# Attention front and step reordered around the norm chain, Newton steps of the inverse norms on GpSimd

## The reference

```python
def _features(x, omega, quad_nodes, quad_weights):
    xn = x / jnp.maximum(jnp.linalg.norm(x, axis=-1, keepdims=True), 1e-12)   # norm of each head's 16 numbers
    proj = jnp.einsum('bhtd,rhdm->rbhtm', xn, omega)
    arg = jnp.clip(proj * sqrt_2s - s, -20.0, 20.0)
    feat = jnp.exp(arg) / np.sqrt(M) * jnp.sqrt(quad_weights)
...
qkv = x @ Wqkv + bqkv
qf, kf = _features(q, ...), _features(k, ...)
# causal sums of k*v and of k over chunks of 128 rows; out = ctx / max(den, 1e-6)
return out @ Wout + bout
```

## Time and profile before

| what | value |
| --- | --- |
| median of 3 runs | 1512.48 us |
| profiled execution | 1517.87 us, span 1516.3 us |
| PE busy | 1378.1 us (91%) |
| DVE, ACT, POOL busy | 914.5, 683.9, 547.4 us |
| mixer phase ends, attention begins | 332.8 us from the span's start |
| steps 1 to 6 of attention | about 62 us each |
| attention ends, shared experts begin | about 819 us |

### The profile page before, as it was taken

The page is one execution under the profiler, slowest core; times in us unless marked ns, Lnnn a source line. Parts: engine busy times, 40 slices in busy tenths (PEclk is TensorE's granted clock), DMA queues, the critical chain, the costliest instruction groups (busy, mean ns, idle before and its releaser), DMA issues. The chain is left out here.

```text
span 1516.3 us, 33677 instructions
## 1 busy us (share of the span) xinstructions
PE 1378.1 (91%) x12000; PEld 1205.1 (79%) x12000; DVE 914.5 (60%) x1944; ACT 683.9 (45%) x1257; POOL 547.4 (36%) x503
## 2 busy tenths in 40 slices
PE   6889999959889789888897998999989999999995
PEld 5778888847667667676676987788889999999984
DVE  4757666758577676676674454344455555555547
ACT  2447756534434444444353432223245555555533
POOL 0235554442234454253410005152324444444431
PEclk7799999969989899898998999899999999999997
DMA  6233441043645545545334322543568888888885
GB/s 239 110 127 111 148 165 57 29 102 99 168 116 162 149 127 153 135 142 152 111 98 155 138 100 99 191 170 142 130 196 229 234 232 233 239 228 234 239 272 204
DMA packets 113085, 241.29 MB, mean 159 GB/s; under 512 B 21616, under 2 KB 77296, under 8 KB 105840
## 3 DMA queue, kind: packets, MB, share of 16 engines
q1 hardware_dynamic: 88768, 185.05, 39.9%
q0 software_dynamic: 23088, 54.31, 12.6%
q10 hardware_dynamic: 1152, 0.93, 0.2%
HBM read 150.23 MB, written 64.84 MB: 142 GB/s over the span
## 5 line engine op out<-in xcount | busy, mean ns | idle before, releaser
L2684 PE MATMUL ps<-e_xhl,s_whl 128*128 128x256 f32 x1848 | 246.9, 283 | 2.0 <-DMA s_whl<-wlo 2.0
L2684 PEld LDWEIGHTS ps<-e_xhl,s_whl 128*128 128x128 f32 x1848 | 232.2, 190 | 2.2 <-issue 2.2
L2066 PE MATMUL ps<-s_xhl,s_whl 128*128 128x512 f32 x660 | 170.3, 406 | 5.3 <-PEq L1127 2.6
L2515 POOL DMA_INDIRECT xs<-e_y,e_slot_id x78 | 122.0, 1564 | 89.3 <-ACT e_y L2549 70.8
L2066 PEld LDWEIGHTS ps<-s_xhl,s_whl 128*128 128x128 f32 x660 | 124.4, 194 | 34.0 <-issue 9.3
L510 POOL TENSOR_TENSOR b_hhl<-b_h,b_hhl 128x512 fp32r<-128x512 f32 x64 | 94.5, 1478 | 139.8 <-ACT b_hhl L774 118.0
L2663 PE MATMUL ps<-s_whl,e_ghl 128*128 128x256 f32 x936 | 139.9, 285 | 0.6 <-issue 0.6
L2763 DVE TENSOR_TENSOR e_g<-ps,e_act_h 128x256 f32<-128x256 f32 x156 | 66.2, 425 | 116.3 <-ACT e_act_h L2562 97.8
L2663 PEld LDWEIGHTS ps<-s_whl,e_ghl 128*128 128x128 f32 x936 | 122.6, 190 | 0.9 <-issue 0.7
L607 PE MATMUL ps<-b_w,b_hhl 128*128 128x256 f32 x768 | 105.3, 287 | 6.3 <-DVE b_turned_rows L880 5.6
L2562 ACT ACTIVATE e_act_h<-ps 128x256 f32<-128x256 f32 x156 | 59.9, 384 | 112.8 <-PE ps L2684 97.6
(11 more groups left out here) (384 smaller groups left out, 2697.2 us busy)
## 6 DMA issues: line engine op xcount, KB each, us to landing
s_whl<-wlo SPq DMA_DIRECT2D x38, 1024.0 KB, 5.1
s_fs<-s_stage SPq DMA_DIRECT2D x192, 128.0 KB, 2.4
s_whl<-wlo SPq DMA_DIRECT2D x38, 512.0 KB
c_eraw<-in_expert_w POOLq DMA_DIRECT2D x24, 512.0 KB, 5.8
wlo<-c_elo POOLq DMA_DIRECT2D x24, 512.0 KB, 3.0
wall<-in_expert_w SPq DMA_DIRECT2D x8, 1536.0 KB
xg<-b_zeros POOLq DMA_DIRECT2D x13, 780.0 KB, 3.9
e_xr<-xg SPq DMA_DIRECT2D x39, 260.0 KB
```

The lines of the kernel that those rows point to most:

```text
L2066: mm = pe.matmul(ps[:, H + 2 * (m % 2) + w, :], whl[:, wp, e, lo:lo + P], xhl[:, k, xp, kd, :], start=q == 0, stop=q == 3 * KD - 1)
L2515: gp.indirect_dma_start(xs, bass.IndirectOffsetOnAxis(ap=slot_id[:, i, b:b + 1], axis=0), y[:, k, b, :], None, compute_op=ALU.add).then_in ...
L2684: mm = pe.matmul(ps[:, H + m, w * SLOT:(w + 1) * SLOT], whl[:, k, wp, lo:lo + P], xhl[:, k, xp, kd, :], start=q == 0, stop=q == 3 * KD - 1)
```

## The change

Five edits. (1) `norm_newton` leaves VectorE; POOL gets `norm_roots` with 12 tensor_tensor on 128x128, and `norm_guess` one more instruction (the product with -0.5). (2) The slots move: FQ 1 to 3 one point earlier, FN 0 and 2 one point earlier, BW and BO 0 later; `squares` go to turn 3 (end) and turn 4 (before mask), with the guess behind the second. (3) The row chain goes from the end of turn 1 to the middle of turn 1, `normalise` from turn 2 to turn 3, `expert_high` from turns 1, 2, 3, 4 to turns 0, 1, 3, 5. (4) In the mixer phase the squares and `next_projected` come earlier and `scale_omega` goes behind the norms. (5) The transposes of the normalised rows and the stack of step 0 go behind the barrier, into a new point Z ahead of turn 0's features, with FV, FT and FQ 0 behind them; the mixer phase loads x2[1] itself and ScalarE does one exp at its end.

```diff
@@ phase_mixer, SP
                 if is_(i, NEXT):
...
-                if is_(i, STEPS + 1):
-                    sp.wait_ge(s["fn_lo"], 2)
-                    for t in range(QUAD):
-                        stack_pair(sp, ahead, t)
+                    sp.wait_ge(s["ft_done"], KD)
+                    sp.dma_start(x0[:], x2[1]).then_inc(x0_in, 16)
@@ phase_mixer, POOL
-                    if is_(i, STEPS) and m in (4, 5):
-                        next_squares(m - 4)
+                    if is_(i, STEPS) and m in (2, 3):
+                        next_squares(m - 2)
@@ phase_mixer, PE: turn_normed removed; ACT
                     act.activation(fc[:, LNA], fc[:, QBIAS], ACT.Ln).then_inc(s["ln_done"], 1)
-                    for c in range(2):
-                        act.wait_ge(s["fn_done"], c + 1)
-                        act.activation(ahead.stage[:, 0, c, :], ps[:, FN_BANK[c], :], ACT.Copy).then_inc(s["fn_hi"], 1)
+                    act.activation(fc[:, UNIT], fc[:, KBIAS], ACT.Exp)
@@ phase_mixer, DVE: next_normed_low removed
                 row_stats(ch, BATCH, N)
+                if is_(i, STEPS):
+                    for b in range(4):
+                        next_projected(b)
...
                 if is_(i, STEPS):
-                    for b in range(2):
-                        next_projected(b)
+                    next_norms()
                     scale_omega()
-                    for b in range(2, 4):
-                        next_projected(b)
-                    next_norms()
@@ phase_attention
-        A_, B_, C_ = range(3)
+        Z_, A_, B_, C_ = range(4)
         SLOTS_OF_X = {0: ((A_, "FN", 1), (B_, "FN", 3), (C_, "BO", 2)),
                       1: ((A_, "BC", 0), (C_, "FV", 0), (C_, "FV", 1)),
-                      2: ((A_, "FT", 0), (A_, "FT", 1), (B_, "BO", 3), (C_, "FQ", 0)),
-                      3: ((A_, "FQ", 1), (B_, "FQ", 2), (C_, "FQ", 3), (C_, "BC", 1)),
-                      4: ((B_, "BW", 0),),
-                      5: ((A_, "BW", 1),),
-                      6: ((A_, "BO", 0), (B_, "FN", 0), (C_, "FN", 2)),
-                      7: ((C_, "BO", 1),)}
+                      2: ((A_, "FT", 0), (A_, "FT", 1), (B_, "BO", 3), (C_, "FQ", 0), (C_, "FQ", 1)),
+                      3: ((A_, "FQ", 2), (B_, "FQ", 3), (C_, "BC", 1)),
+                      4: (),
+                      5: ((C_, "BW", 0),),
+                      6: ((A_, "FN", 0), (B_, "FN", 2), (C_, "BW", 1)),
+                      7: ((A_, "BO", 0), (C_, "BO", 1))}
+        FIRST_OF_X = {0: ((Z_, "FM", 0), (Z_, "FM", 1), (Z_, "FV", 0), (Z_, "FV", 1), (Z_, "FT", 0), (Z_, "FT", 1), (Z_, "FQ", 0),
+                          (A_, "FN", 1), (B_, "FN", 3), (C_, "FQ", 1)),
+                      1: ((A_, "FQ", 2), (B_, "FQ", 3)),
...
+                      6: ((A_, "FN", 0), (B_, "FN", 2)),
+                      7: ((A_, "BO", 0), (C_, "BO", 1))}
@@ SP
+            stack(0, 0)
+            for n in range(2):
+                load_shared(n)
...
+                if is_step(i + 1):
+                    stack(i + 1, 0)
                 if is_step(i - 1) and (not isinstance(i, int) or i < STEPS):
                     sp.wait_ge(s["x_free"], x_index(i, "BW", 1) + 1)
                     sp.dma_start(xb[:], x2[i]).then_inc(s["res_in"], 16)
-                if is_step(i + 1):
-                    stack(i + 1, 0)
@@ POOL
                     split_expert_weights(i, range(2, EPER - 1))
                 if is_step(i + 1):
+                    norm_roots(i)
                     for c in range(KD):
-                        gp.wait_ge(s["rnorm_ready"], f)
...
+            def norm_roots(i):
+                ch = Chain(gp, s["norm_root"], 4 * 3)
...
+                for n in range(3):
+                    ch.link(gp.tensor_tensor(nt, nr, nr, ALU.mult))
+                    ch.link(gp.tensor_tensor(nt, nt, nv, ALU.mult))
+                    ch.link(gp.tensor_tensor(nt, nt, three_halves[:, 0:1].to_broadcast([P, BATCH * 2 * HEADS1]), ALU.add))
+                    ch.link(gp.tensor_tensor(nr, nt, nr, ALU.mult))
@@ POOL, start: the three memsets of va and state come before the loads of eraw
@@ ACT
-                    if t == 2 and is_step(i - 2) and not last_rows(i):
+                    if t == 3 and is_step(i - 2) and not last_rows(i):
                         normalise(i - 1)
                     x_high(i, t, C_)
...
-                    if 1 <= t <= EPER and (not isinstance(i, int) or 1 <= i < LAST):
-                        expert_high(i, t - 1)
+                    if t in EXPERT_AT and (not isinstance(i, int) or 1 <= i < LAST):
+                        expert_high(i, EXPERT_AT.index(t))      # EXPERT_AT = (0, 1, 3, 5)
@@ DVE, body(i), turn t
                     x_evac(i, t, A_)
                     if front and t == 4:
-                        squares(norm, i + 1, 0)
-                    if front and t == 5:
-                        norm_newton(norm, False)
+                        squares(norm, i + 1, 1)
+                        norm_guess(norm)
...
+                    if is_step(i - 2) and not last_rows(i) and t == 1:
+                        ...
+                        row_moments(rows)
                     x_evac(i, t, B_)
                     if pair(i, t, 2) is not None:
                         new_state(*pair(i, t, 2))
-                    if front and t == 5:
-                        norm_newton(norm, False)
-                        norm_newton(norm, True)
-                        norm.end()
+                    if is_step(i - 2) and not last_rows(i) and t == 1:
+                        row_guess(rows)
                     x_evac(i, t, C_)
-                    if front and t == 4:
-                        squares(norm, i + 1, 1)
-                        norm_guess(norm)
+                    if front and t == 3:
+                        squares(norm, i + 1, 0)
```

More of the change, by code:

```diff
@@ L339, in phase_mixer @@
         NEXT = STEPS - 1
-        FT_BANK, FQ_BANK, FN_BANK = (1, 3), (0, 2, 1, 3), (0, 2)
+        FT_BANK, FQ_BANK = (1, 3), (0, 2, 1, 3)
         WQ, WO = KD * 3 * D, KD * D
         omr = w2raw[:, 0:PAIRS * P]
-        HIGH, LOW, KBIAS, QBIAS, AMP, LNA, NONE = (slice(n, n + 1) for n in range(7))
+        HIGH, LOW, KBIAS, QBIAS, AMP, LNA, NONE, UNIT = (slice(n, n + 1) for n in range(8))
         def is_(i, n):
@@ L1122, in phase_mixer, with phase_attention @@
     nc.all_engine_barrier()
-def phase_attention(nc, x2, bout, masks, x3, routed_w, wlo, ps, ids, rows_out, x2_stored, x3_stored, early, x0, fc, ahead, shared_w):
+def phase_attention(nc, x2, x0_in, bout, masks, x3, routed_w, wlo, ps, ids, rows_out, x2_stored, x3_stored, early, x0, fc, ahead, shared_w):
     with ExitStack() as ctx:
@@ L1201, in x_list @@
         def x_list(i):
-            return [(t, point, name, a) for t in range(PAIRS) for point, name, a in SLOTS_OF_X[t] if is_step(step_of(i, name, a))]
+            slots = FIRST_OF_X if isinstance(i, int) and i == 0 else SLOTS_OF_X
+            return [(t, point, name, a) for t in range(PAIRS) for point, name, a in slots[t] if is_step(step_of(i, name, a))]
         def x_before(i, kinds):
@@ L1266, in load_shared @@
                 sp.dma_start(ahead.raw[:, n * CC:(n + 1) * CC], swf[:, n * CC:(n + 1) * CC]).then_inc(ahead.raw_in[n], 16)
-            for n in range(2):
-                load_shared(n)
             def stack(i, half):
-                k1 = (i, "FN", 3) if half else (i - 1, "FN", 2)
+                k1 = (i, "FN", 3) if half else (0, "FM", 1) if isinstance(i, int) and i == 0 else (i - 1, "FN", 2)
                 sp.wait_ge(s["x_free"], x_index(*k1) + 1)
@@ L1363, in _ @@
             mean, v, r, t_, nb = (small[:, k, :] for k in (0, 2, 3, 4, 5))
+            def norm_roots(i):
+                ch = Chain(gp, s["norm_root"], 4 * 3)
+                ch.turn(i)
+                gp.wait_ge(s["guessed"], i + 1)
+                gp.wait_ge(s["norm_own"], 5 * (i + 1))
+                nv, nr, nt = (nrm[:, k, :] for k in range(3))
+                for n in range(3):
[3 more added lines that the diff above has]
+                    ch.link(gp.tensor_tensor(nr, nt, nr, ALU.mult))
+                ch.end()
             def row_roots(i):
@@ L1416, in x_step @@
                     if a == 0:
-                        pe.wait_ge(s["x_in"], 16 * step)
+                        if isinstance(i, int) and i == 0:
+                            pe.wait_ge(x0_in, 32)
+                        else:
+                            pe.wait_ge(s["x_in"], 16 * i)
                     for b in range(BATCH):
@@ L1426, in x_step @@
                                     lambda p, kd: wq[:, p, kd, 2 * D:3 * D], KD)
+                elif name == "FM":
+                    for b in range(BATCH):
+                        mm = pe.transpose(ps[:, xp, b * P:(b + 1) * P], sq[:, b, 2 * a * P:(2 * a + 1) * P], ids[:])
                 elif name == "FN":
@@ L1544, in high_of @@
         def high_of(name, a):
+            if name == "FM":
```

(19 more changed lines are left out.)

46 lines of the change are left out of this document (17 added, 29 removed).

## The result

The kernel after takes 1506.78 us (median of 20 runs) beside 1514.72 us of the kernel before (20 runs on the same chips): ratio 0.994, 95% interval 0.9924 to 0.9956. That is 7.9 us faster. The forecast was 16.5 to 16.9: the sign is right, the size is half. The profiled execution took 1503.63, span 1502.0, so the two profiled executions differ by 14.2, more than the medians; 10.8 of it lies before the end of attention, 3.5 in later phases that the change doesn't touch.

A forecast was written before the change was run, and what follows sets the result against it. Attention was taken as bound by a closed loop through the stack DMAs, 62.1 us a step. Gains of 14.4 (middle steps), 2 (front) and 0.5 (last step) sum to 16.9: 1512.5 to 1495.6, said as 1496, range 1481 to 1508.

The forecast's parts named there:

- The loop: Attention step: 11.5 us from stack DMA start to FN 1's copy, plus 50.6 to the next stack start, makes 62.1.
- Path of the middle steps: Steps 1 to 6, FN 1's copy to next stack start: 3.4 us shorter, less clock loss, taken as 2.4 a step.
- Newton: Twelve 128x128 instructions on GpSimd in each middle step take 6.1 us, against 6.3 on VectorE; bounds 3.4 and 16.4.
- both new PE waits: Middle steps: PE idles 1.7 us before turn 5's features (late clip) and 2.6 before turn 4's scores (mask).
- FN 0 waits for POOL and not for PE: Middle steps, turn 6: PE waits from 553.7 to 555.1 for the normalised rows, the argument that new stalls cost little.
- the new stalls eat the gain: Rival, chance 0.15: PE stalls in turns 3 to 5 leave 0 to 1 us a step, 1504 to 1511 us.
- the chain itself does not get shorter: Middle steps: moving the Newton instructions to GpSimd keeps their span, only relieving VectorE of about 2.9 us.
- The landing of the middle steps: Time from stack start to FN 1's copy, left at 11.5 us although chunk 3's DMAs come just behind the stack.
- The rival of the late landing: Chance 0.10: FN 2 comes earlier but chunk 3's 1 MB delays the stack's landing, up to 1.5 us a step, 1503.
- Step 0: First attention step: the next step's stack starts 1.8 us earlier, taken as 2, between -1 and 6.
- The phase did begin earlier than forecast: End of the mixer phase: attention begins at 326.2 instead of 332.8, 6.6 us earlier, between 3 and 10.
- Last step: No norm chain there; turn 2's clip no longer waits for the row chain, gaining 0.5 us.

The follow-up runs named there:

- the run with both repairs of the middle steps: Kernel after with normalise in turn 2, chunk 3 behind the next step's xb sum, squares 0 and expert_high 2 earlier in turn 3: ratio 0.9765 to the kernel before.

## Why the prediction was half right

- **The loop** (landing + path = step) is how the runs were read, and single edits moved one term or the other; the two are not independent, as the run with both repairs of the middle steps shows.
- **Path of the middle steps**: forecast -2.4 a step, measured -2.26. Several parts were right too: Newton 6.08 us (forecast 6.1) at 0.40 and 0.46 an instruction, both new PE waits at 1.58 and 2.54 (forecast 1.7 and 2.6), scores at 2.08 behind them. Others were off and cancel, which is luck. I had products at 0.41 and the sum with 1.5 at 0.47; measured, the sum takes 0.40, and 0.46 is the price of the two products whose inputs are different tiles. The guess came 2.8 earlier relative to FN 1's copy in the step shown and 2.4 in the mean, not 1.6; and FN 0, which my sum had waiting for the rows (553.7 to 555.1), came behind them by 1.3 in the mean. "FN 0 waits for POOL and not for PE", my case against the rival that the new stalls eat the gain (chance 0.15), no longer holds in the new order. That rival is partly what happened, and 1506.8 lies within its times: the run with the normalise in turn 2 took 2.1 of path back.
- **Newton**: "the chain itself does not get shorter" is right for the old order and there the edit even costs 0.35%. It misses what it does beside the reordering: without it the reordered kernel is slower than before (1.0107). I costed the two edits one by one on the old trace.
- **The landing of the middle steps is the first failed step**, a term that I left as it was: "Chunk 3's two DMAs of 512 KB, issued just before the stack starts now, come just behind it, so I leave the 11.5 as it is." It rose by 0.51 a step, 3.1 us in six. The rival of the late landing, to which I gave 0.10, is what happened too, and its price is visible from both sides: 9.5 without chunk 3, 13 to 15 on top of it. Even the 11 of before held 1.5 us of it, which I took for the stack's own time. The alternation of short and long steps has to do with it. Behind the landings of 12.9, 12.6 and 12.6 PE is 1.1, 2.7 and 2.8 late at FN 0, and the next stack starts 1.4, 2.8 and 3.1 behind chunk 3's store and lands sooner; behind those of 11.2 and 10.0 PE is 0.6 late, and the next stack starts 0.7 behind the store and lands in 12.6. Why a late landing should make PE late was not tested, and in the run with the normalise in turn 2 PE reached FN 0 in time behind a landing of 14.7, so it stays open.
- **Step 0 is the second, and the larger**: forecast stack of step 1 1.8 earlier, measured 2.3 later, 4.1 off; by itself the front costs 0.28%. The phase did begin earlier than forecast (10.3 against 6.6). One reason is VectorE, which ended the norms at 313.9 where my sum had 316.8. But phase begin to stack took 57.8 us, where my sum gives 45.15 + 4.8 = 50. The 7.8 have two parts. FN 1's copy came 17.0 behind the begin instead of 15.2, 1.8 more: the landing was 13.7, since GpSimd's first loads start at 325.78 with the stack at 325.79. And from that copy to the next stack it took 40.8 us, where 43.1 of before less 6.3 and 2 gives 34.8, 6.0 more: I let the 6.3 us of FV, FT and FQ 0 taken out of turns 1 and 2 come off in full, though squares and guess keep their place in turns 3 and 4, so that PE waits instead. This 6.0 is the largest single miss. The run with the chain in turn 2, FN 0 in turn 4 and the loads held back shows both together: from begin to stack 41.8 instead of 58.2. FV at the lower clock is in neither part; PE waited 4.16 behind it.
- **Last step**: 2.5 shorter, forecast 0.5. It makes up 2 of the loss; no run took it apart.

The terms of the trace: 6 x (2.26 - 0.51) - 2.3 + 2.5 = 10.7 against 16.9. The medians give 7.9; the 2.8 between is not explained by any term, and the 20 executions of the kernel after lie between 1498.88 and 1513.32.

## What to carry to other kernels

When a loop is closed by a burst of DMAs, its landing is a term like any other: before shortening the path, list which other transfers the new start will meet, and read from the old trace how the landing depends on that distance. A wait that is long is not a wait that costs: taking away a PE stall brings nothing if the chain that PE meets next comes later for it, and an edit worth nothing by itself can be what lets another one pay. Work that is taken out of a turn brings little while the chain that ends the step keeps its turn.

## What the runs showed of the hardware

Two 512 KB transfers issued by GpSimd lengthen the landing of twelve 128 KB stack DMAs issued by SP from 9.5 us to between 13.3 and 15.2 when the store starts with the stack or up to 0.4 us behind it, and to 10 when it starts 2.8 us ahead. With the load cut to 1/16 and the store starting with the stack the landing is 10.4 and 10.7. The profile's median from issue to landing of one stack DMA, which is taken over all 192 of them, follows this only in part: 3.6 us after, 4.0 in the run with early squares, 2.4 with chunk 3 late, but 2.4 before too. On GpSimd a 128x128 tensor_tensor took 0.40 with a product of a tile with itself or a sum with a broadcast, 0.46 with two different tiles. At 128x1024 it is alike: 1.9 for a square or a product with a broadcast, 2.4 for a difference of two tiles. Dependent ones stood 0.08 from end to start of the next.
